# Queries and keys in five stages of seven block products for two groups, and a shorter rounding and closing step

## Chip, core and metric

The kernel runs on one core of one Trainium2 chip. The metric is device time in microseconds (us), as the median of several runs; lower is better. The core has five engines with a queue each: TensorE (PE) multiplies matrices into eight banks of PSUM, VectorE (DVE) and ScalarE (ACT) work element by element, GpSimd (POOL) does too but reaches no PSUM, and SyncE (SP) issues the transfers. An engine works through its queue in order; engines wait for each other on semaphores.

## What is computed

The input x has 32 batches of 32 rows with 512 columns. Each batch picks one of 16 conditions, whose 32x32 matrix mixes the batch's rows (h). On h runs causal attention with 32 query heads, 8 key and value heads and head size 128, with rotary positions. A second mixing and an fp8-rounded linear layer follow. Cut to what matters:

```python
h = einsum('bct,bcd->bdt', x, cond_weights[itok])
q, k, v = h @ wq, h @ wk, h @ wv                  # 32, 8 and 8 heads of 128
q = q*cos + rotate_half(q)*sin;  k likewise
att = softmax(mask(q @ k.T / sqrt(128)))          # four query heads share a key head
x = x + (att @ v) @ wo
y = einsum('bct,bcd->bdt', x, cond2_weights[itok])
s = amax(abs(y)) / 448;  a = fp8_round(y / s) * s # fp8 e4m3
f = a @ (fp8_round(qweight) * weight_scale).T + bias
so = amax(abs(f)) / 448
out = x + clip(f / so, -448, 448) * so
```

## The kernel before

**Layout.** The 1024 rows of x are 8 tiles of 128 rows, or two halves of 512 rows; `xacc` holds them to the end. The transposed h stands as `hT`. Every large product takes three passes of fp32r matmuls over a high and a low part of both operands (`_hi`, `_lo`: ACT rounds the high part, DVE or POOL subtracts it to get the low one); a pass over 128 contracted values and 512 columns is one matmul. All of them are issued at lines 733 to 735 (`three_pass`).

**Groups.** One key head with its four query heads is a group; there are eight. A group has two halves of program, `half(g, 0)` and `half(g, 1)`, written once for each engine. In a half PE makes the group's keys for 512 rows directly (`key`: 4 chunks x 3 passes = 12 matmuls), and two query heads for all 1024 rows as a 2x2 block product with seven block products in place of eight (`product` 0 to 6, 6 matmuls each; POOL sums the weight blocks in `sum_weights`; DVE joins the products in PSUM with seven `block_sum` steps). Each finished block of 128x512 (an item) is rotated: ACT swaps its halves (`swap`), DVE multiplies by cosine and sine (`rope`), POOL adds the two (`rope_add`). There are two `q_swap` buffers, so ACT's swap of item k+2 waits for POOL's addition of item k. Only one `wq_hi`/`wq_lo` set exists: while the products of a half run, ACT (`q_high`) and POOL (`q_low`) write the next half's seven parts over those already used.

**Attention.** `scores(g, r)` multiplies keys and queries of row half r once all items of the group have been added by POOL. DVE transposes them (`turn_scores`) and does the softmax in seven steps (`soft` 0 to 6, with ACT's `exponent` between 2 and 3); step 6 writes `p_tr`. `attend(g, r)` multiplies `p_tr` with the values, ACT and DVE split the outcome into `o_hi` and `o_lo` (`o_high`, `o_low`), and `project_out(g, r, j)` multiplies tile j of four with `wo` (12 matmuls), which DVE adds to `xacc` (`accumulate`). ACT and POOL split `wo` of a group (`wo_high`, `wo_low`, four heads) once the group before has been projected. One group and row half is a unit.

**Order.** The order in each queue is written out by hand, and the loop runs over groups 2 to 6. A half on PE is: key, attend of an older unit, seven products, three projected tiles of that unit, scores (second half of a group only), the fourth tile. While products of groups 0 and 1 run, the value product (`values`, 16 tiles) is still being finished and takes the place of projection. On DVE a half is: `soft` 0 to 2, the key's `rope`, four `o_low`, then block sums, `soft` 3 and 4, four ropes and the additions between each other, with `soft` 5 and 6 behind the last rope.

**The end.** After the last projection, `y_largest` finds the maximum of y, PE spreads it over partitions (`spread_max`), and for each of 8 tiles ACT scales y twice (`y_div`, `y_exp`), DVE turns `y_exp` into a power of two with bit operations (`magic`, line 1266), adds and subtracts it (lines 1286 and 1295, which rounds to fp8's steps), PE multiplies (`f_mm`) and DVE takes the maximum (`f_largest`). Then ACT divides each tile (line 652), DVE clips it (line 1319) and adds it back to `xacc` (line 1324), and SP stores it. `hold_clock` issues matmuls whose results nobody reads.

Of the kernel before, what the change touches and what calls it, by code (L numbers as in the profile page):

```python
# [7 lines left out]
F32 = mybir.dt.float32  # L8
# [19 lines left out]
ITEMS = 1 + REP  # L28
# [14 lines left out]
V_BEFORE = (9, 11, 15, 16)  # L43
# [35 lines left out]
def build(nc, x, itok, conds, wq, wk, wv, wo, qweight, w_scale, bias, consts, v_mem, out):  # L79
    with ExitStack() as ctx:  # L80
# [19 lines left out]
        with ExitStack() as products:  # L100
# [17 lines left out]
            with ExitStack() as steady:  # L118
                q_rot = sb("q_rot", [P, 2, REP, HALF], F32, steady)
                k_rot = sb("k_rot", [P, 2, HALF], F32, steady)  # L120
# [14 lines left out]
                wk_lo = sb("wk_lo", [P, KC, HD], F32R, steady)  # L135
# [3 lines left out]
                raw_q = sb("raw_q", [P, 2, KC, 2 * HD], F32, steady)  # L139
                raw_k = sb("raw_k", [P, KC, HD], F32, steady)  # L140
# [37 lines left out]
        dma_q = [sem(f"dma_q{i}") for i in range(2)]  # L178
        dma_k, dma_o, dma_out = sem("dma_k"), sem("dma_o"), sem("dma_out")
# [12 lines left out]
        w8_scaled, w8_step, wT_mm, wT_done = sem("w8_scaled"), sem("w8_step"), sem("wT_mm"), sem("wT_done")  # L192
        y_mm, y_copied, y_amax, tail_mm, tail_vec = (sem(n) for n in ("y_mm", "y_copied", "y_amax", "tail_mm", "tail_vec"))
        y_div_done, y_exp_done, y8_magic, y8_sum, y8_done = (
            sem(n) for n in ("y_div_done", "y_exp_done", "y8_magic", "y8_sum", "y8_done"))
# [26 lines left out]
        wv_raw = [raw_o[:], raw_q[:].rearrange("p s c n -> p (s c n)").rearrange("p (c n) -> p c n", n=HID)]  # L222
# [10 lines left out]
        bias_row = raw_k[0:BIAS_ROWS].rearrange("p c n -> p (c n)")  # L233
        bias_sc = k_rot[0:BIAS_ROWS, 0, :]
        bias_parts = wk_hi[0:BIAS_ROWS].rearrange("p c n -> p (c n)")
        y_div = lambda t: y_divs[:, t, :]
        y_exp = lambda t: wv_raw[1][:, t, :] if t < TPU else raw_o[:, t - TPU, :]
        f_div = y_exp
        f_keep = second_u[:]
        y_t = lambda t: y_kept[:, t, :] if t < TPU else y_ps[t][:]  # L240
        y_sum = [flat(p_tr), flat(s_nat[0])]
        tmp_scaled = [second_u[:], third_u[:]]
        tmp_sum = first_p[:]

        def left_part(h, i):

            a11, a12 = raw_q[:, h, 0:2, 0:HD], raw_q[:, h, 2:4, 0:HD]
            a22 = raw_q[:, h, 2:4, HD:2 * HD]
            return (a11, w_sum[:, 1], w_sum[:, 2], a12, w_sum[:, 0], a22, w_sum[:, 3])[i]

        def item_out(h, k):
            return k_rot[:, h, :] if k == 0 else q_rot[:, item_row[k - 1], 2 * h + item_head[k - 1], :]

        def unit_of(g, h):

            return (g - 2, 1) if h == 0 else (g - 1, 0)

        late = [range(V_BEFORE[n], V_BEFORE[n + 1]) for n in range(3)]

# [4 lines left out]
        def _(sp):  # L264

# [11 lines left out]
            sp.dma_start(raw_k[:], wk_v[:, :, 0:HD]).then_inc(dma_k, 16)  # L277
# [5 lines left out]

            def load_pair(g, h):
                sp.dma_start(raw_q[:, h], wq_v[:, :, bass.ds((2 * g + h) * 2 * HD, 2 * HD)]).then_inc(dma_q[h], 16)
# [7 lines left out]
            load_pair(0, 0)  # L293
            store_values(2)
            store_values(3)
            load_pair(0, 1)
# [6 lines left out]
            def half(g, h, last):  # L303

                n = 2 * g + h
                if not (isinstance(g, int) and g == KV - 1):
                    sp.wait_ge(wq_lo_done, PRODUCTS * (n + 1))
                    load_pair(g + 1, h)
                    if h == 0:
                        sp.wait_ge(wk_lo_done, g + 1)  # L310
                        sp.dma_start(raw_k[:], wk_v[:, :, bass.ds((g + 1) * HD, HD)]).then_inc(dma_k, 16)
                if h == 0 and not (isinstance(g, int) and g < 2):
                    sp.wait_ge(wo_lo_done, (g - 1) * REP)
                    sp.dma_start(raw_o[:], wo_v[:, bass.ds((g - 1) * REP, REP), :]).then_inc(dma_o, 16)
                if not (isinstance(g, int) and n < 2):
                    if not (isinstance(g, int) and n < 4):
                        sp.wait_ge(pv_mm, BPT * (n - 3))
                    load_values(g - 1, h)

            half(0, 0, None)  # L320
            for i in late[0]:
                store_values(i)
            half(0, 1, None)
            for i in late[1]:
                store_values(i)
            for i in range(V_SLOTS):
                sp.wait_ge(dma_v[i], 16 * len(range(i, V_BEFORE[2], V_SLOTS)))
            half(1, 0, None)
            for i in late[2]:
                store_values(i)  # L330
            for i in late[2]:
                sp.wait_ge(dma_v[i % V_SLOTS], 16 * (i // V_SLOTS + 1))
            half(1, 1, (0, 0))
            with sp.Fori(2, KV - 1) as g:
                half(g, 0, unit_of(g, 0))
                half(g, 1, unit_of(g, 1))
            half(KV - 1, 0, unit_of(KV - 1, 0))
            half(KV - 1, 1, unit_of(KV - 1, 1))

            sp.wait_ge(prod_mm, PRODUCTS * 2 * KV)  # L340
            sp.dma_start(raw_w8[:], qw_v).then_inc(dma_ffn, 16)
            sp.wait_ge(wk_lo_done, KV)
# [3 lines left out]
            for r in range(2):  # L346
                sp.wait_ge(pv_mm, BPT * (2 * (KV - 2) + r + 1))
                load_values(KV - 1, r)

            for t in range(TILES):  # L350
                sp.wait_ge(result, t + 1)
                sp.dma_start(out_rows[t], xacc[:, t, :]).then_inc(dma_out, 16)
# [4 lines left out]
        def _(pool):  # L357
            def sum_weights(g, h):

                n = 2 * g + h  # L360
                pool.wait_ge(dma_q[h], 16 * (g + 1))
                if isinstance(g, int) and n == 0:
# [3 lines left out]
                a11, a12 = raw_q[:, h, 0:2, 0:HD], raw_q[:, h, 2:4, 0:HD]  # L366
                a21, a22 = raw_q[:, h, 0:2, HD:2 * HD], raw_q[:, h, 2:4, HD:2 * HD]
# [7 lines left out]
            def q_low(g, h, i):  # L375
                n = PRODUCTS * (2 * g + h) + i
                pool.wait_ge(wq_hi_done, n + 1)
                pool.tensor_tensor(wq_lo[:, i], left_part(h, i), wq_hi[:, i].bitcast(F32), ALU.subtract).then_inc(wq_lo_done, 1)  # L378

# [21 lines left out]
            for i in range(PRODUCTS):  # L401
                q_low(0, 0, i)
# [957 lines left out]
```

## Time and profile before

| | |
|---|---|
| median of 3 runs | 521.12 us (521.07 to 521.58) |
| profiled execution, its own time | 521.22 us |
| its span, first to last instruction | 519.3 us |
| PE busy | 501.1 us (96%) |
| DVE busy | 418.6 us (81%) |
| POOL busy | 310.2 us (60%) |
| ACT busy | 248.2 us (48%) |
| TensorE clock granted, mean over the span | 0.991 |

The profiled execution took 0.10 us more than the median of the runs, and 1.92 us of its time lie outside the span. Busy counts time in which an instruction of the engine was under way; matmuls are pipelined, so the recorded length of one (about 390 ns) is longer than the distance between two.

### The profile page before, as it was taken

Reading aid. Unit: us, or ns where it says so; the run is one execution under the profiler, and the core shown is the slowest. Engines: PE = TensorE matmul, PEld = TensorE weight load, DVE = VectorE, ACT = ScalarE, POOL = GpSimd, SP = SyncE. Lnnn points to the kernel's source line nnn. Section 1 sums busy time; section 2 is a strip of 40 time slices with the busy share of each in tenths; the row PEclk is TensorE's granted clock in tenths of the full one; section 3 lists DMA queues with packets and bytes.
Section 4 is the critical chain, followed back from the end, with each engine's and each line's share of the span. In section 5 each row is a group of like instructions: output and inputs, shape, how many; then the busy total and the mean of one; then the engine's idle time right before and its main releaser. Section 6 shows DMA issues by size and latency. Waiting matters only on the chain.

```text
span 519.3 us, 9226 instructions
## 1 busy us (share of the span) xinstructions
PE 501.1 (96%) x3148; PEld 401.5 (77%) x3150; DVE 418.6 (81%) x662; ACT 248.2 (48%) x475; POOL 310.2 (60%) x308
## 2 busy tenths in 40 slices
PE   8999999999999999999999999999999999999990
PEld 6888888877888888888888888888888887788530
DVE  5468967899688877978797879787978798985896
ACT  2652644564446453735472637263726354232523
POOL 0668688888669746884788388838874754200000
PEclk9999999999999999999999999999999999999996
DMA  7346111320502050104010410131300014000004
GB/s 263 140 145 204 41 62 62 101 82 1 163 1 62 1 162 1 59 3 158 10 51 13 149 33 27 39 122 57 104 1 21 1 43 168 0 2 1 0 0 162
DMA packets 32644, 35.27 MB, mean 68 GB/s; under 512 B 2251, under 2 KB 22859, under 8 KB 32620
## 3 DMA queue, kind: packets, MB, share of 16 engines
q1 hardware_dynamic: 32620, 34.96, 21.1%
q8 instruction: 14, 0.23, 0.2%
q14 instruction: 10, 0.08, 0.0%
HBM read 28.66 MB, written 6.29 MB: 67 GB/s over the span
## 4 chain that ended last, share of the span: by engine, by line
PE 89%; DVE 4%; POOL 3%; issue 1%; DMA 1%; ACT 0%; DVEq 0%; ACTq 0%; SPq 0%; POOLq 0%
PE bank L733 23%; PE bank L734 22%; PE bank L735 22%; PE bank L803 3%; PE bank L792 3%; PE bank L705 3%; PE bank L706 3%; PE bank L707 3%; PE bank L676 1%; POOL q_rot L392 1%; PE bank L861 1%; PE bank L938 1%; POOL wq_lo L378 1%; PE bank L687 1%; DVE xacc L1324 1%
## 5 line engine op out<-in xcount | busy, mean ns | idle before, releaser
L392 POOL TENSOR_TENSOR q_rot<-q_rot,q_swap 128x512 f32<-128x512 f32 x64 | 88.2, 1377 | 60.9 <-DVE q_swap L1070 60.9
L521 ACT ACTIVATE q_swap<-bank 64x512 f32<-64x512 f32 x80 | 47.7, 596 | 124.3 <-PE bank L735 76.9
L733 PE MATMUL bank<-wo_hi,o_hi 128*128 128x512 f32 x256 | 101.4, 396 | 0.8 <-issue 0.6
L734 PE MATMUL bank<-wo_lo,o_hi 128*128 128x512 f32 x256 | 99.8, 390 | 0.0
L735 PE MATMUL bank<-wo_hi,o_lo 128*128 128x512 f32 x256 | 99.7, 390 | 0.0
L1118 DVE TENSOR_TENSOR xacc<-xacc,bank 128x512 f32<-128x512 f32 x64 | 43.7, 683 | 35.8 <-PE bank L735 35.7
L1070 DVE TENSOR_TENSOR q_swap<-q_swap,cst 128x512 f32<-128x512 f32 x80 | 60.2, 752 | 0.0
L733 PEld LDWEIGHTS bank<-wo_hi,o_hi 128*128 128x128 f32 x256 | 48.1, 188 | 13.1 <-issue 2.6
L735 PEld LDWEIGHTS bank<-wo_hi,o_lo 128*128 128x128 f32 x256 | 48.1, 188 | 10.2
L734 PEld LDWEIGHTS bank<-wo_lo,o_hi 128*128 128x128 f32 x256 | 48.1, 188 | 9.5
L387 POOL TENSOR_TENSOR wo_lo<-raw_o,wo_hi 128x512 fp32r<-128x512 f32 x32 | 45.5, 1444 | 9.5 <-ACT wo_hi L507 9.5
L733 PE MATMUL bank<-t_hi,wq_hi 128*128 128x512 f32 x128 | 49.9, 390 | 0.4 <-DVE o_lo L1111 0.4
L734 PE MATMUL bank<-t_lo,wq_hi 128*128 128x512 f32 x128 | 49.8, 389 | 0.0
L735 PE MATMUL bank<-t_hi,wq_lo 128*128 128x512 f32 x128 | 49.8, 389 | 0.0
L378 POOL TENSOR_TENSOR wq_lo<-w_sum,wq_hi 128x256 fp32r<-128x256 f32 x64 | 48.0, 761 | 1.6 <-ACT wq_hi L490 1.6
L522 ACT ACTIVATE q_swap<-bank 64x512 f32<-64x512 f32 x80 | 47.3, 591 | 0.9
L1069 DVE TENSOR_TENSOR q_rot<-bank,cst 128x512 f32<-128x512 f32 x64 | 43.9, 686 | 2.9 <-ACT q_swap L522 1.3
L378 POOL TENSOR_TENSOR wq_lo<-raw_q,wq_hi 128x256 fp32r<-128x256 f32 x48 | 38.4, 800 | 7.1 <-ACT wq_hi L490 7.1
L1111 DVE TENSOR_TENSOR o_lo<-bank,o_hi 128x512 fp32r<-128x512 f32 x64 | 39.6, 679 | 2.7 <-ACT o_hi L538 2.7
L392 POOL TENSOR_TENSOR k_rot<-k_rot,q_swap 128x512 f32<-128x512 f32 x16 | 20.8, 1298 | 34.1 <-DVE q_swap L1070 34.1
L538 ACT ACTIVATE o_hi<-bank 128x512 fp32r<-128x512 f32 x64 | 33.1, 604 | 16.4 <-PE bank L803 16.1
L733 PE MATMUL bank<-hT_hi,wq_hi 128*128 128x512 f32 x96 | 38.9, 405 | 0.0
(160 smaller groups left out, 1042.3 us busy)
## 6 DMA issues: line engine op xcount, KB each, us to landing
raw_q<-in_L_attn_wq SPq DMA_DIRECT2D x16, 512.0 KB, 4.0
raw_o<-in_L_attn_wo SPq DMA_DIRECT2D x8, 1024.0 KB, 7.0
v_st<-values SPq DMA_DIRECT2D x16, 256.0 KB, 4.4
xacc<-in_x SPq DMA_DIRECT2D x4, 512.0 KB, 7.5
raw_k<-in_L_attn_wk SPq DMA_DIRECT2D x8, 256.0 KB, 4.3
out<-xacc SPq DMA_DIRECT2D x8, 256.0 KB, 2.0
values<-v_more SPq DMA_DIRECT2D x6, 256.0 KB, 2.1
raw_o<-in_L_attn_wv SPq DMA_DIRECT2D x1, 1024.0 KB, 8.1
```

The costliest lines, as they stand in the source:

```text
L378: pool.tensor_tensor(wq_lo[:, i], left_part(h, i), wq_hi[:, i].bitcast(F32), ALU.subtract).then_inc(wq_lo_done, 1)
L387: pool.tensor_tensor(lo[:, h, :], raw_o[:, h, :], hi[:, h, :].bitcast(F32), ALU.subtract).then_inc(wo_lo_done, 1)
L392: pool.tensor_tensor(item_out(h, k), item_out(h, k), q_swap[(h + k) % 2][:], ALU.add).then_inc(rope_done, 1)
L521: act.activation(dst[0:P // 2, :], ps[P // 2:P, :], ACT.Copy)
L522: act.activation(dst[P // 2:P, :], ps[0:P // 2, :], ACT.Copy).then_inc(swap_done, 1)
L733: pe.matmul(dst, l_hi, r_hi, start=(i == 0), stop=False)
L734: pe.matmul(dst, l_hi, r_lo, start=False, stop=False)
L735: mm = pe.matmul(dst, l_lo, r_hi, start=False, stop=(i == n - 1))
L1069: dve.tensor_tensor(by_t(item_out(h, k)), by_t(item_ps[k][:]), cos_b, ALU.mult).then_inc(rope_cos, 1)
L1070: dve.tensor_tensor(by_t(q_swap[b][:]), by_t(q_swap[b][:]), sin_b, ALU.mult).then_inc(rope_mul, 1)
L1111: dve.tensor_tensor(by_batch(lo, b), by_tile(ps[b]), by_batch(hi, b).bitcast(F32), ALU.subtract).then_inc(o_lo_done, 1)
L1118: dve.tensor_tensor(xacc[:, tile, :], xacc[:, tile, :], w_ps[j % 2][:], ALU.add).then_inc(acc_done, 1)
```

## The change

Two groups now share five stages in place of four halves. A stage is one block product of seven with two heads' columns; the ten columns are eight query heads and the two keys, so `key`, `k_high` and `k_low` are gone. Stage 0 holds the even group's key (`k_first`) and its query head 0, stage 1 its heads 1 and 2, stage 2 its head 3 and the odd group's key (`k_second`), stages 3 and 4 the odd group's heads. `p` counts pairs of groups; the even group's scores follow in stage 2 (`side=0`), the odd group's in stage 4 (`side=1`). Attention and projection of older units are spread anew over the stages, stage 1 having no `attend`. `raw_q` has three slots, and stages 0 and 2 load their two columns with two transfers.

At the end ACT's absolute value, written as bfloat16, replaces the bit operations. Four f tiles are copied off PSUM early; PE adds `xacc` and the scaled result of tiles 2, 4 and 6 in PSUM with an identity matrix (`place_old`, `scaled_ident`) and ACT copies the sum to `xacc`; the clipping order and store order are written out anew. One `hold_clock` matmul stands where three stood.

```diff
-            for i in range(PRODUCTS):
-                q_low(0, 0, i)
-            k_low(0)
...
+            def stage(p, i, split_wo=None):
                 if more:
-                    sum_weights(*follow)
...
+                    sum_weights(*following(p, i))
+                if split_wo is not None:
                     for head in range(REP):
...
+                        wo_low(split_wo, head, wo_lo)
                 if more:
...
+                    for m in range(4):
+                        q_low(*following(p, i), m)
+                for k in range(ITEMS):
+                    rope_add(p, i, k)
                 if more:
...
+                    for m in range(4, PRODUCTS):
+                        q_low(*following(p, i), m)
+
+            def stages(p):
+                stage(p, 0)
+                stage(p, 1)
+                stage(p, 2, split_wo=None if isinstance(p, int) and p == 0 else 2 * p - 1)
+                stage(p, 3)
+                stage(p, 4, split_wo=2 * p)
...
+            def stage(p, i, last=None, fill=(), ahead=(), behind=(), end=(), side=None):
+                n = STAGES * p + i
+                for tile in ahead:
+                    project_out(*tile)
                 if last is not None:
-                    pe.wait_ge(rope_cos, 5 * n)
+                    pe.wait_ge(rope_cos, ITEMS * n)
+                    if i in (0, 3):
+                        pe.wait_ge(s_turned, 4 * p + (0 if i == 0 else 2) - 1)
                     attend(*last)
...
+                products_of(p, i, last)
+                for tile in fill:
+                    values(tile)
+                for tile in behind:
+                    project_out(*tile)
+                if side is not None:
+                    scores(p, side, 0)
+                    scores(p, side, 1)
+                for tile in end:
+                    project_out(*tile)
...
+                stage(p, 0, last=(2 * p - 2, 1), ahead=tiles(2 * p - 2, 0, 3), behind=tiles(2 * p - 2, 1, 0, 1))
+                stage(p, 1, behind=tiles(2 * p - 2, 1, 2, 3))
+                stage(p, 2, last=(2 * p - 1, 0), behind=tiles(2 * p - 1, 0, 0, 1, 2), side=0, end=tiles(2 * p - 1, 0, 3))
+                stage(p, 3, last=(2 * p - 1, 1), behind=tiles(2 * p - 1, 1, 0, 1, 2))
+                stage(p, 4, last=(2 * p, 0), ahead=tiles(2 * p - 1, 1, 3), behind=tiles(2 * p, 0, 0, 1, 2), side=1)
+
+            stage(0, 0, fill=late[0])
+            stage(0, 1, fill=late[1])
+            stage(0, 2, fill=late[2], side=0)
+            stage(0, 3, fill=late[3])
+            stage(0, 4, last=(0, 0), behind=tiles(0, 0, 0, 1, 2), side=1)
...
+                stage(p, 0, last=(2 * p - 2, 1), weights=(2 * p - 1, 0), steps=range(3), ahead=tiles(2 * p - 2, 0, 3),
+                      behind=tiles(2 * p - 2, 1, 0, 1))
+                stage(p, 1, weights=(2 * p - 1, 0), steps=range(3, SOFT_STEPS), behind=tiles(2 * p - 2, 1, 2, 3))
...
+            stage(0, 3, weights=(0, 0), fill=late[3])
...
-            def magic(t):
...
-                dve.tensor_scalar(y_exp(t).bitcast(I32), y_exp(t).bitcast(I32), EXP_BITS, HALF_BIT,
-                                  ALU.bitwise_and, ALU.bitwise_or).then_inc(y8_magic, 1)
...
+                    pe.matmul(f_ps[n + 1][:, part], ident, xacc[:, BY_PE[n], part], start=(c == 0), stop=False)
...
+                    mm = pe.matmul(f_ps[n + 1][:, part], scaled_ident, f_div(t)[:, part], start=False, stop=(c == KC - 1))
```

The first `stage` is POOL's, the second (from `last=None, fill=()` on) PE's, the calls with `weights` DVE's. `late` holds value tiles 9 and 10, 11 and 12, 13 and 14, 15 for the stages (0, 0) to (0, 3). The softmax of unit (2p-1, 0) is split: `soft` 0 to 2 in stage 0 and 3 to 6 in stage 1. That of unit (0, 0), which stood whole at the end of `half(0, 1)`, is spread over stage (0, 3).

The first place is DVE's queue where a part of the program ends with a softmax (`xacc` rows are `accumulate`, `p_tr` is `soft` 6, `s_nat1` rows the next unit's `soft` 0 to 2, bank6 and bank7 the two banks of projection). Before, from the last rope of `half(7, 0)` to the start of the next half:

```order
L1069 TENSOR_TENSOR q_rot<-bank4,cst 128x512
L1070 TENSOR_TENSOR q_swap0<-q_swap0,cst 128x512
L1098 TENSOR_TENSOR s_nat0<-s_exp,s_rec 128x512
L1118 TENSOR_TENSOR xacc<-xacc,bank7 128x512
L1105 STREAM_TRANSPOSE p_tr<-s_nat0 128x512
L1118 TENSOR_TENSOR xacc<-xacc,bank6 128x512
...
L1086 TENSOR_TENSOR s_nat1<-s_nat1,cst 128x512
```

Of the change, from the last rope of stage 1 of the last pair to the start of stage 2:

```order
L1098 TENSOR_TENSOR q_rot<-bank4,cst 128x512
L1099 TENSOR_TENSOR q_swap1<-q_swap1,cst 128x512
L1127 TENSOR_TENSOR s_nat0<-s_exp,s_rec 128x512
L1147 TENSOR_TENSOR xacc<-xacc,bank7 128x512
L1134 STREAM_TRANSPOSE p_tr<-s_nat0 128x512
L1115 TENSOR_TENSOR s_nat1<-s_nat1,cst 128x512
```

The rows up to `p_tr` are alike, but the bank7 row now takes in the last projected tile of its unit, and PE's next work is the `attend` that reads `p_tr`; before, two more tiles (the bank6 row and another) and a key stood between on PE.

The second place is POOL's queue ahead of the rope additions (rows that write `q_rot`, `k_rot` or `k_second`). Before, in `half(g, 1)` of the loop:

```order
L373 TENSOR_TENSOR w_sum<-raw_q,w_sum 128x256
...
L387 TENSOR_TENSOR wo_lo<-raw_o,wo_hi 128x512
...
L392 TENSOR_TENSOR k_rot<-k_rot,q_swap1 128x512
...
L378 TENSOR_TENSOR wq_lo<-raw_q,wq_hi 128x256
...
L392 TENSOR_TENSOR q_rot<-q_rot,q_swap0 128x512
```

Of the change, in stage 2 of the last pair:

```order
L415 TENSOR_TENSOR w_sum<-raw_q,w_sum 128x256
L424 TENSOR_TENSOR wo_lo<-raw_o,wo_hi 128x512 x4
L419 TENSOR_TENSOR wq_lo<-raw_q,wq_hi 128x256
L419 TENSOR_TENSOR wq_lo<-w_sum,wq_hi 128x256 x2
L419 TENSOR_TENSOR wq_lo<-raw_q,wq_hi 128x256
L428 TENSOR_TENSOR q_rot<-q_rot,q_swap0 128x512
L428 TENSOR_TENSOR k_second<-k_second,q_swap1 128x512
```

Before, two `wo_lo` stood on either side of the key's addition, and three additions in a row came behind the first of a query head. Now all four `wo_lo` and four `wq_lo` stand ahead of the first of four additions.

## Rows read from the trace of the kernel before

**Rows 1.** The page: span, then busy time of each engine.

```profile
span 519.3 us, 9226 instructions
PE 501.1 (96%) x3148; PEld 401.5 (77%) x3150; DVE 418.6 (81%) x662; ACT 248.2 (48%) x475; POOL 310.2 (60%) x308
```

**Rows 2.** Windows: stretch, length, busy PE, PEld, DVE, ACT, POOL; clock, DMA, GB/s.

```profile
46.24:129.12 82.88, 82.25 (x497) 66.92 (x495) 70.22 (x103) 43.31 (x84) 67.55 (x67) 1.00 0.22 68
...
231.19:282.19 51.00, 51.00 (x334) 41.72 (x333) 42.50 (x67) 26.01 (x51) 36.35 (x38) 1.00 0.18 57
```

**Rows 3.** Timeline of PE, `half(g, 1)` in the loop: start, length, instruction.

```profile
261.23 1.17 PE L803 MATMUL bank<-p_tr,v_st 32*128 32x128 f32 x32
262.33 0.50 PE L733 MATMUL bank<-hT_hi,wq_hi 128*128 128x512 f32 x1
...
271.99 0.39 PE L733 MATMUL bank<-wo_hi,o_hi 128*128 128x512 f32 x1
...
280.24 1.96 PE L792 MATMUL bank<-q_rot,k_rot 128*32 128x128 f32 x64
```

**Rows 4.** Timeline of DVE in that half (in brackets idle time and releaser).

```profile
268.11 0.70 DVE L1050 TENSOR_TENSOR bank<-bank,first_p 128x512 f32<-128x512 f32 x1 [0.19 <-PE bank L735]
...
277.25 0.69 DVE L1070 TENSOR_TENSOR q_swap<-q_swap,cst 128x512 f32<-128x512 f32 x1
...
279.07 0.70 DVE L1105 STREAM_TRANSPOSE p_tr<-s_nat 128x512 f32<-128x512 f32 x1
```

**Rows 5.** Timeline of POOL in that half.

```profile
260.66 2.99 POOL L387 TENSOR_TENSOR wo_lo<-raw_o,wo_hi 128x512 fp32r<-128x512 f32 x2
...
265.79 2.56 POOL L387 TENSOR_TENSOR wo_lo<-raw_o,wo_hi 128x512 fp32r<-128x512 f32 x2 [0.23 <-ACT wo_hi L507]
268.31 0.74 POOL L378 TENSOR_TENSOR wq_lo<-raw_q,wq_hi 128x256 fp32r<-128x256 f32 x1
269.01 1.43 POOL L378 TENSOR_TENSOR wq_lo<-w_sum,wq_hi 128x256 fp32r<-128x256 f32 x2
...
272.17 1.29 POOL L392 TENSOR_TENSOR q_rot<-q_rot,q_swap 128x512 f32<-128x512 f32 x1 [1.03 <-DVE q_swap L1070]
...
278.02 1.68 POOL L392 TENSOR_TENSOR q_rot<-q_rot,q_swap 128x512 f32<-128x512 f32 x1 [0.63 <-DVE q_swap L1070]
```

**Rows 6.** Timeline of DVE ahead of the first key.

```profile
47.86 2.89 DVE L1001 TENSOR_TENSOR t_lo<-t_full,t_hi 128x1024 fp32r<-128x1024 f32 x2
```

**Rows 7.** Timeline of DVE in the rounding of y and the closing step.

```profile
498.17 0.68 DVE L1286 SCALAR_TENSOR_TENSOR s_nat<-raw_o,y_divs 128x512 f32<-128x512 f32 x1
498.77 0.42 DVE L1266 TENSOR_SCALAR raw_o<-raw_o 128x512 int32<-128x512 int32 x1
499.10 0.69 DVE L1295 SCALAR_TENSOR_TENSOR y<-raw_o,s_nat 128x512 bf16<-128x512 f32 x1
...
500.31 0.68 DVE L1286 SCALAR_TENSOR_TENSOR p_tr<-raw_o,y_divs 128x512 f32<-128x512 f32 x1
...
508.49 1.00 DVE L1319 TENSOR_SCALAR raw_q<-raw_q 128x512 f32<-128x512 f32 x2 [0.79 <-ACT raw_q L652]
...
515.40 1.41 DVE L1324 SCALAR_TENSOR_TENSOR xacc<-raw_o,col,xacc 128x512 f32<-128x512 f32 x2
```

**Rows 8.** DMA issues: size, us to landing.

```profile
raw_q<-in_L_attn_wq SPq DMA_DIRECT2D x16, 512.0 KB, 4.0
...
out<-xacc SPq DMA_DIRECT2D x8, 256.0 KB, 2.0
```

**Rows 9.** Windows in the closing step, columns as in rows 2.

```profile
517.00:518.00 1.00, 0.00 (x0) 0.00 (x0) 0.00 (x0) 0.00 (x0) 0.00 (x0) 0.50 1.00 373
```

**Rows 10.** Windows around PE's last matmul.

```profile
506.70:510.20 3.50, 0.00 (x0) 0.00 (x0) 2.44 (x8) 2.46 (x5) 0.00 (x0) 1.00 0.00 0
510.20:519.30 9.10, 0.00 (x0) 0.00 (x0) 6.60 (x13) 2.31 (x4) 0.00 (x0) 0.50 0.61 231
```

**Rows 11.** Timeline of PE at the start of the program.

```profile
1.46 4.28 PE L664 MATMUL bank<-warm 128*128 128x512 bf16 x11 [1.46 <-DVE warm L946]
```

More of the change, by code:

```diff
@@ L243, in build @@
         tmp_sum = first_p[:]
[L245 to L258, printed above, removed]
+        SLOT = (0, 1, 0, 1, 2)
@@ L334, in _ @@
[L334 to L340, printed above, removed]
+            stage(0, 4)
+            with sp.Fori(1, PAIRS - 1) as p:
+                for i in range(STAGES):
+                    stage(p, i)
+            for i in range(STAGES):
+                stage(PAIRS - 1, i)
+            sp.wait_ge(prod_mm, PRODUCTS * STAGES * PAIRS)
@@ L597, in _ @@
+            stage(0, 0)
+            stage(0, 1)
+            stage(0, 2)
+            stage(0, 3, soft=(0, 0))
+            stage(0, 4, last=(0, 0), soft=(0, 1), split_wo=0)
+            with act.Fori(1, PAIRS - 1) as p:
+                stages(p)
+            stages(PAIRS - 1)
             for b in range(BPT):
@@ L1118, in accumulate, with stage, soft_part @@
                 dve.tensor_tensor(xacc[:, tile, :], xacc[:, tile, :], w_ps[j % 2][:], ALU.add).then_inc(acc_done, 1)
-            def half(g, h, last=None, weights=None, fill=(), fill_last=(), soft_first=None):
-                def soft_part(*steps):
-                    if weights is not None:
-                        for step in steps:
+            def stage(p, i, last=None, weights=None, steps=range(SOFT_STEPS), fill=(), ahead=(), behind=(), end=(), side=None):
+                def soft_part(*some):
+                    for step in some:
+                        if weights is not None and step in steps:
                             soft(*weights, step)
-                def add_out(j):
-                    if last is not None:
-                        accumulate(*last, j)
                 soft_part(0, 1, 2)
-                rope(g, h, 0)
+                for tile in ahead:
+                    accumulate(*tile)
                 if last is not None:
@@ L1183, in round_w8 @@
+            dve.wait_ge(dma_const, 32)
+            stage(0, 0, fill=late[0])
+            stage(0, 1, fill=late[1])
+            stage(0, 2, fill=late[2], side=0)
+            stage(0, 3, weights=(0, 0), fill=late[3])
+            stage(0, 4, last=(0, 0), weights=(0, 1), behind=tiles(0, 0, 0, 1, 2), side=1)
+            with dve.Fori(1, PAIRS - 1) as p:
+                stages(p)
+            stages(PAIRS - 1)
             def round_w8(c):
```

618 lines of the change are left out of this document (301 added, 317 removed).

## The prediction

> **What bounds the kernel now.** The page first: PE is busy for 501.1 of 519.3 us and DVE for 418.6 [rows 1], so PE is full and DVE is next. Then the windows: a group of the loop takes 51.00 us and PE is busy for all of them; in the opening, from the first key to the tile behind group 1's scores, PE idles for 0.63 of 82.88 us [rows 2]. So a matmul less is time less, unless PE then waits. Third the timelines of one half of the loop, from which I take the durations and, more important, how far the other engines trail PE. I call P the start of a stage's first product, 262.33 in that half.
>
> PE [rows 3]: an `attend` of 32 small matmuls holds it for 1.1 us (261.23 to 262.33). The seven products, 42 matmuls, take 9.66 (262.33 to 271.99), 0.23 each. Three projected tiles take 8.25 (271.99 to 280.24), 2.75 each. So scores start at P+17.91.
>
> DVE [rows 4]: its third block sum still waits for PE at 268.11, P+5.78. From there 19 more instructions stand with hardly a gap between them, at about 0.60 from start to start, up to `soft` 6, which begins at 279.07 and lasts 0.70: `p_tr` is ready at P+17.44. The sine of the last rope stands at 277.25, P+14.92.
>
> POOL [rows 5]: the four query additions run from 272.17 (P+9.84) to 279.70 (P+17.37), 7.53 us, since each pair of `q_swap` buffers goes round through POOL, ACT and DVE. A first addition that is late therefore makes the last one late by as much. The last one ends 0.54 us ahead of the scores.
>
> Today both are covered: behind `p_tr` PE has two tiles and a key (in the first half of a group), or scores, a tile and the next key. The question is what covers them in the new order.
>
> **Removed.** 16 halves of 54 matmuls become 20 stages of 42: 864 less 840, 24 matmuls, at 0.23 that is 5.5 us, or 1.38 for each of the four pairs of groups.
>
> **Added and hidden.** 28 block sums at 0.60 are 17 us more of DVE, some 4.2 in a pair of groups; POOL gets 28 `wq_lo` and 16 weight sums at 0.70 (from 268.31 to 269.01 [rows 5]), less 8 `wk_lo`. In the loop DVE is busy for 42.5 of 51.0 and POOL for 36.4 [rows 2], so neither becomes full, and this costs nothing as busy time; it matters where it stands in a queue, below. Two 256 KB loads replace one of 512 KB that lands in 4.0 us [rows 8]; they are issued a stage (over 15 us) ahead and stay hidden even at twice that.
>
> **Waits in a steady pair (p = 1 to 3).** Stage 1 has no `attend` and only two tiles: PE has 9.66 + 5.50 = 15.16 us of work, then comes the `attend` that reads the `p_tr` of this same stage. DVE's rows up to `soft` 6 are the same as before, so it ends at P+17.44 at the earliest: PE waits 2.3, with the signal 2.4. Lower bound 1.7, if one 0.60 step less is in the way; upper bound 3.5, if POOL's additions are late here too. Behind this `attend` everything of PE is queued.
>
> Stage 2: POOL comes from the last addition of stage 1 (P+17.37 there), about as `attend` starts, and has three `wq_lo` (2.1), four weight sums (2.8 at the same 0.70), four `wo_low` at 1.28 (5.1, half of 265.79's 2.56) and four `wq_lo` (2.8) ahead of the first addition: 12.8, so to P+11.6 of stage 2 after 1.1 of `attend`. The natural time is P+9.84. The last addition ends at 11.6 + 7.53 = P+19.1, and PE is at the scores at P+17.9: 1.2. Bounds 0 (if the loop's slack of 1.76 took it up) and 2.4 (contended, rival C).
>
> Stage 4: the same POOL work, with a tile of 2.75 ahead of `attend`, but the splitting of `wo` may only start behind that tile. Between 0 and 1.2; I take 0.9, since the start of the splitting moves back as well. In the last pair no next weights stand ahead, so there it is 0. Stages 0 and 3 use a `p_tr` from a stage earlier: no wait.
>
> So 2.4 + 1.2 + 0.9 - 1.38 = +3.1 for a pair, three pairs less the last 0.9: **+8.4**.
>
> **Waits in the opening (pair 0).**
> - Product 1 of stage (0, 0) reads the third part of `t_lo`. Two parts take 47.86 to 50.75 [rows 6], so the third ends at about 49.3. Before, PE began at 46.24 [rows 2] with a key (12 x 0.23 = 2.8) and product 0 (1.4), so product 1 came at 50.4. Now product 1 comes at 47.6: 1.7.
> - Stage (0, 2): products and two value tiles take 15.16, then scores want POOL's last addition of this stage, P+17.37: 2.2.
> - The first product of stage (0, 3) uses the bank of the second scores and waits for DVE's transpose of it (0.70 and a signal): 0.9, where a projected tile lies between otherwise.
> - Stage (0, 3): products and one value tile, 12.41. Then `attend(0, 0)` wants `soft` 6 of this stage. One DVE step fewer than in the row's half stands ahead of it, so P+16.8: **4.4**, the largest single wait.
> - Stage (0, 4): POOL is 0.5 later against `attend` than in stage 2, so 1.8 at the scores by the same sum.
>
> Together 11.0, less 1.38 and the 0.6 that PE idles there today: **+9.0** (bounds +5 and +11, with 0 and 2.4 for the POOL waits and 2.5 to 5 for the 4.4).
>
> **The end.** DVE makes a y tile in 2.14 (498.17 to 500.31), of which the bit operation is 0.33 (498.77 to 499.10) [rows 7]. Without it over six tiles on the path: -2.0. ACT's absolute value takes the place of a pass that it made already, and the bfloat16 input has no row; I take DVE's 0.60 for it as for fp32 (half of it would give 4 us more over the end). In the closing step DVE now has seven or eight clips and five additions in place of eight and eight, 0.33 and 0.67 (1.00 a tile from 508.49 to 515.40), so its last result is some 4.5 earlier in all. But the stores: 256 KB at 373 GB/s [rows 9] is 0.70, six of eight are then queued behind each other, and each lands in 2.0 [rows 8]. The end moves from 519.3 to about 516.3: **-3.0**, with bounds of -1.5 and -5.
>
> **Sum.** 519.3 + 9.0 + 8.4 - 3.0 = 533.7 span, + 1.92 outside = 535.6 us for the profiled execution; the median of runs lay 0.10 below it, so 535.5.
>
> **Rivals.** *A*, the sum above.
>
> *B, the clock.* PE's last matmul ends at 506.7, the granted clock stays at 1.00 (2.4 GHz) to 510.2 and is then 0.50 (1.2 GHz) [rows 10]. The wait of 4.4 in stage (0, 3) is longer than these 3.5 us. The 11 first matmuls of the program took 4.28 us [rows 11] where 11 at 0.23 are 2.5: a fall costs about 1.8. Then 537.3. The Trainium skill ("TensorE: Matmul & The Clock Gate", Part 1) calls the throttled clock the default that activity releases; rows 10 agree. Against B: at the end nothing follows at all, while here PE stands between dense stages.
>
> *C, POOL slower.* At 260.66 two `wo_lo` took 2.99 in place of 2.56, and the addition at 278.02 took 1.68 in place of 1.29, while DVE worked on two SBUF operands [rows 5]. If all POOL work of stages 2, 4 and (0, 4) is 1.17 times as long, 12.8 becomes 15.0: +2.2 at three stages 2, two stages 4 and (0, 4), less what the bounds above leave free, some 1.2 each: +7, 542.5. The Trainium skill ("GPSIMD Engine Reference", section 1) says that POOL's SBUF interfaces are shared with VectorE and that instructions with two SBUF inputs contend; the 1.68 beside 1.29 agrees.
>
> *D, faster: DVE does not trail.* The chain of 20 DVE instructions starts at P+5.8 behind the third block sum and would be short enough: without `soft` 0 to 2 and `o_low` ahead of it in stages 1 and (0, 3), and with POOL's additions in step, each wait falls below what PE's work covers. Then only -5.5, the t_lo wait and the end count: 521.1 - 5.5 + 1.7 - 3.0 = 514.3. It decides if the waits, 24 in my sum (11.0 + 3 x 4.5 - 0.9), come to less than 8.5. Against it: 19 of 20 steps stand gapless at 0.60 in rows 4 although PE's sums were ready; that is what P+17.4 is made of.
>
> *E, no change:* waits of just 8.5; nothing speaks for that in particular.
>
> **Chances.** A 0.63 (530 to 540 for itself), B 0.14, C 0.08, D 0.11, E 0.04. The range 526 to 541 takes in A's bounds (opening +5, pairs with only the 2.4 left, end -5: about 524; upper bounds about 541) and B, and leaves out D and most of C. 0.2%, 1 us, is about what a measurement of this kernel can tell from no change: faster 0.11, same 0.04, slower 0.85.
>
> **What would show it.** Right: PE busy falls by some 5 us while the span grows; waits of PE's first `attend` matmuls for DVE's `p_tr`, 4.4 once at stage (0, 3) to (0, 4) and 2.4 in each later pair; waits of the scores for POOL's `q_rot`, `k_second`; a pair of groups taking about 105 in place of 102.0. Wrong: `soft` 6 of stage 1 ending before P+15.2, POOL's first addition of stage 2 at P+10, a granted clock under 1.00 before the end, or stores of the end that leave DMA idle between them.

## The result and the profile after

| | before | changed |
|---|---|---|
| median | 521.35 us (521.07 to 521.74, 4 runs) | 550.51 us (547.80 to 550.80, 4 runs) |
| profiled execution | 521.22 us, span 519.3 | 547.80 us, span 546.0 |

The changed kernel takes 1.0549 times as long (95% interval 1.052 to 1.0578). Slower was forecast, but by half of that: 535.5 us, with 541 as the upper bound. The profiled execution is the fastest of the changed kernel; the others had a mean granted clock of 0.969 to 0.974 where this one has 0.979, so the rows below show rather too little of the loss. All sums here are made against the profiled execution.

From the page of the changed kernel (as [rows 1], with the granted clock in 40 slices):

```profile
span 546.0 us, 9233 instructions
PE 509.6 (93%) x3160; PEld 408.1 (75%) x3160; DVE 429.6 (79%) x676; ACT 259.2 (47%) x505; POOL 334.1 (61%) x344
PEclk9999999889999799999998999999989999999999
```

PE has 24 matmuls of the products fewer (in the closing step the trace has 48 small ones more and 12 of `hold_clock` fewer) and is yet busy for 8.5 us longer: the slices of 8 and 7 in the clock's line hold the stretches in which it ran at half speed. Where the time went is read off the start of the odd groups' scores. In the timeline of PE before, group 1's and group 7's:

```profile
127.24 1.96 PE L792 MATMUL bank<-q_rot,k_rot 128*32 128x128 f32 x64
...
433.24 1.95 PE L792 MATMUL bank<-q_rot,k_rot 128*32 128x128 f32 x64
```

and of the changed kernel, of groups 1, 3, 5 and 7:

```profile
139.74 1.95 PE L800 MATMUL bank<-q_rot,k_second 128*32 128x128 f32 x64
...
248.10 1.95 PE L800 MATMUL bank<-q_rot,k_second 128*32 128x128 f32 x64
...
356.34 1.96 PE L800 MATMUL bank<-q_rot,k_second 128*32 128x128 f32 x64
...
463.08 1.95 PE L800 MATMUL bank<-q_rot,k_second 128*32 128x128 f32 x64
```

PE's first matmul for keys and queries starts at 46.24 in the profiled executions of both. So the opening is 12.5 us longer (forecast 9.0). The pairs of groups take 108.4, 108.2 and 106.7 in place of 102.0: +6.4, +6.2 and +4.7 (forecast 3.1, 3.1 and 2.2). From the last scores to the end there are 82.9 in place of 86.1 us: -3.1 (forecast -3.0). Together 26.7, which is the difference of the spans.

The waits of PE in the changed kernel (line and tile that waited, who released it: us in all, times, longest):

```profile
PE bank L811 <- DVE p_tr L1134: 13.5, 4, 4.6
PE bank L748 <- DVE xacc L1147: 6.1, 5, 1.7
PE bank L800 <- POOL q_rot L428: 3.4, 1, 3.4
```

The first row is the `attend` behind stage 1 of each later pair and that behind stage (0, 3). The second is not in the forecast: a projected tile that waits until DVE has taken the tile before last out of its bank. The third is group 0's scores. On PE they look like this (timeline; in brackets the idle time and its releaser):

```profile
95.97 3.19 PE L800 MATMUL bank<-q_rot,k_first 128*32 128x128 f32 x64 [3.37 <-POOL q_rot L428]
...
117.14 2.09 PE L811 MATMUL bank<-p_tr,v_st 32*128 32x128 f32 x32 [4.61 <-DVE p_tr L1134]
...
178.75 2.09 PE L811 MATMUL bank<-p_tr,v_st 32*128 32x128 f32 x32 [2.87 <-DVE p_tr L1134]
...
245.03 0.50 PE L748 MATMUL bank<-wo_hi,o_hi 128*128 128x512 f32 x1 [1.25 <-DVE xacc L1147]
```

These two `attend` take 2.09 us; in [rows 3] it took 1.17. The windows around those places (columns as in [rows 2], the granted clock third from the end) show why:

```profile
96.00:100.00 4.00, 3.17 (x64) 2.70 (x64) 1.50 (x3) 0.00 (x0) 3.86 (x6) 0.57 0.36 99
117.00:121.00 4.00, 3.86 (x38) 3.36 (x39) 3.83 (x5) 1.78 (x4) 3.86 (x5) 0.57 0.02 4
178.00:184.00 6.00, 5.25 (x40) 4.34 (x41) 5.93 (x9) 2.33 (x5) 5.84 (x8) 0.54 0.26 79
184.00:186.00 2.00, 2.00 (x8) 1.57 (x7) 0.07 (x2) 2.00 (x5) 1.51 (x2) 0.69 0.62 170
186.00:192.00 6.00, 6.00 (x28) 4.96 (x27) 4.64 (x9) 3.98 (x9) 6.00 (x7) 1.00 0.01 3
```

The clock goes to its lower level, 1.2 GHz, behind each of the waits for `p_tr` and behind that of group 0's scores, and comes back some 3 to 7 us later. That happens five times ahead of the end, once in each pair and twice in the opening, not at most once as in the forecast.

POOL from stage 1 to stage 2 of pair 1 (timeline, as [rows 5]):

```profile
176.96 1.65 POOL L428 TENSOR_TENSOR q_rot<-q_rot,q_swap 128x512 f32<-128x512 f32 x1 [0.63 <-DVE q_swap L1099]
...
184.93 5.06 POOL L424 TENSOR_TENSOR wo_lo<-raw_o,wo_hi 128x512 fp32r<-128x512 f32 x4 [0.49 <-ACT wo_hi L528]
189.93 0.76 POOL L419 TENSOR_TENSOR wq_lo<-raw_q,wq_hi 128x256 fp32r<-128x256 f32 x1
190.63 1.46 POOL L419 TENSOR_TENSOR wq_lo<-w_sum,wq_hi 128x256 fp32r<-128x256 f32 x2
192.04 1.21 POOL L419 TENSOR_TENSOR wq_lo<-raw_q,wq_hi 128x256 fp32r<-128x256 f32 x1
193.20 1.30 POOL L428 TENSOR_TENSOR q_rot<-q_rot,q_swap 128x512 f32<-128x512 f32 x1
```

From the end of stage 1's last addition (178.6) to stage 2's first (193.2) POOL works for 14.6 us with hardly a gap, where the forecast put 12.8.

### The profile page after: what moved, and what is told of

It reads as the page before. It is cut to its first block, busy times and chain, and to the rows that moved or that the text cites. A ratio compares the mean times of both kernels' runs of the same rounds, so it can differ in the third digit from the quotient of the medians.

```text
span 546.0 us, 9233 instructions
## 1 busy us (share of the span) xinstructions
PE 509.6 (93%) x3160; PEld 408.1 (75%) x3160; DVE 429.6 (79%) x676; ACT 259.2 (47%) x505; POOL 334.1 (61%) x344
## 4 chain that ended last, share of the span: by engine, by line
PE 50%; POOL 21%; DVE 13%; issue 11%; ACT 2%; DMA 1%; POOLq 0%; DVEq 0%; ACTq 0%; SPq 0%
PE bank L748 13%; PE bank L750 12%; PE bank L749 12%; POOL q_rot L428 8%; POOL wq_lo L419 6%; DVE q_swap L1099 4%; PE bank L800 3%; POOL wo_lo L424 3%; PE bank L811 2%; PE bank L720 2%; PE bank L722 2%; PE bank L721 1%; ACT q_swap L538 1%; PE bank L691 1%; DVE q_rot L1098 1%
## 5 line engine op out<-in xcount | busy, mean ns | idle before, releaser
L419 POOL TENSOR_TENSOR wq_lo<-raw_q,wq_hi 128x256 fp32r<-128x256 f32 x60 | 48.5, 809 | 34.1 <-ACT wq_hi L517 34.1
L419 POOL TENSOR_TENSOR wq_lo<-w_sum,wq_hi 128x256 fp32r<-128x256 f32 x80 | 63.7, 806 | 2.2 <-ACT wq_hi L517 2.1
L748 PE MATMUL bank<-t_hi,wq_hi 128*128 128x512 f32 x160 | 63.1, 394 | 1.0 <-DVE t_lo L1031 1.0
L749 PE MATMUL bank<-t_lo,wq_hi 128*128 128x512 f32 x160 | 62.8, 392 | 0.0
L750 PE MATMUL bank<-t_hi,wq_lo 128*128 128x512 f32 x160 | 62.6, 391 | 0.0
L1099 DVE TENSOR_TENSOR q_swap<-q_swap,cst 128x512 f32<-128x512 f32 x80 | 61.8, 772 | 0.0
L748 PE MATMUL bank<-hT_hi,wq_hi 128*128 128x512 f32 x120 | 50.0, 417 | 0.9 <-issue 0.9
L424 POOL TENSOR_TENSOR wo_lo<-raw_o,wo_hi 128x512 fp32r<-128x512 f32 x32 | 41.4, 1328 | 14.8 <-ACT wo_hi L528 14.8
L749 PE MATMUL bank<-hT_lo,wq_hi 128*128 128x512 f32 x120 | 48.5, 404 | 0.0
L750 PE MATMUL bank<-hT_hi,wq_lo 128*128 128x512 f32 x120 | 48.0, 400 | 0.0
```

What stands on the lines that cost most here:

```text
L419: pool.tensor_tensor(wq_lo[:, m], left_part(i, m), wq_hi[:, m].bitcast(F32), ALU.subtract).then_inc(wq_lo_done, 1)
L424: pool.tensor_tensor(lo[:, h, :], raw_o[:, h, :], hi[:, h, :].bitcast(F32), ALU.subtract).then_inc(wo_lo_done, 1)
L748: pe.matmul(dst, l_hi, r_hi, start=(i == 0), stop=False)
L749: pe.matmul(dst, l_hi, r_lo, start=False, stop=False)
L750: mm = pe.matmul(dst, l_lo, r_hi, start=False, stop=(i == n - 1))
L1099: dve.tensor_tensor(by_t(q_swap[b][:]), by_t(q_swap[b][:]), sin_b, ALU.mult).then_inc(rope_mul, 1)
```

## The experiments

Two theories stood at the start. The first is the forecast's: the late `p_tr` costs its wait, and as the clock now shows, a fall of the clock besides; take it away and both come back. The second: another queue, POOL's or DVE's, sets the length of a pair, and a wait that is removed comes back elsewhere. Unless it is said otherwise, a kernel below computes all that the changed kernel does and differs by the lines shown. The comparisons are with the kernel before, run on the same chip.

**e1: the softmax early**

```diff
+                if i == 1:
+                    for step in early:
+                        soft(*weights, step)
                 soft_part(0, 1, 2)
...
                 block_sum(p, i, 0)
+                if i == 3:
+                    for step in early:
+                        soft(*weights, step)
                 block_sum(p, i, 1)
...
-                stage(p, 1, weights=(2 * p - 1, 0), steps=range(3, SOFT_STEPS), behind=tiles(2 * p - 2, 1, 2, 3))
+                stage(p, 1, weights=(2 * p - 1, 0), steps=range(3, SOFT_STEPS), early=range(3, SOFT_STEPS), behind=tiles(2 * p - 2, 1, 2, 3))
```

> DVE does soft 3 to 6 of unit (2p-1, 0) as the first thing in stage 1, where it idles for 2.0 us at present, and those of unit (0, 0) behind the first block sum of stage (0, 3); nothing else changes. If p_tr at the end of DVE's queue is what PE waits for, and the clock's falls come from that wait, then the waits of 3.0, 3.0 and 3.3 us in the loop shrink to the 0.7 us by which the last rope's cosine trails PE's tiles, the one of 4.8 us to about 2.7, and the slow attend and products behind them (1.6 to 3.0 us each) go: 550.5 becomes about 535 us. If DVE or POOL are simply too busy (the rival), the wait comes back at the accumulation or at the scores, and the time stays over 546.

Measured: 550.92 us, 1.0555 times before (1.0538 to 1.0573): nothing gained. Yet the wait for `p_tr` is gone, as the timeline of PE in pair 1 shows, from the end of stage 1 on (the last row is in stage 4):

```profile
180.53 1.17 PE L811 MATMUL bank<-p_tr,v_st 32*128 32x128 f32 x32 [1.10 <-DVE q_rot L1098]
...
185.37 0.49 PE L748 MATMUL bank<-t_hi,wq_hi 128*128 128x512 f32 x1 [0.72 <-DVE o_lo L1140]
...
193.93 0.49 PE L748 MATMUL bank<-wo_hi,o_hi 128*128 128x512 f32 x1 [1.47 <-POOL wo_lo L424]
...
201.45 0.50 PE L748 MATMUL bank<-wo_hi,o_hi 128*128 128x512 f32 x1 [1.79 <-DVE xacc L1147]
...
248.71 0.50 PE L748 MATMUL bank<-wo_hi,o_hi 128*128 128x512 f32 x1 [1.26 <-DVE xacc L1147]
```

and so is the fall of the clock, in the window of the same kernel:

```profile
178.00:184.00 6.00, 4.90 (x49) 3.82 (x48) 5.90 (x9) 3.97 (x9) 4.58 (x5) 1.00 0.00 0
```

PE arrives in stage 2 earlier and waits there three times, 4.0 us together, for `o_low`, `wo_low` and the accumulation. A pair still takes 108.5 us (scores at 143.27 and 251.78). The first theory falls: the wait and the fall were real, but something behind them was as late. POOL, in the same kernel:

```profile
180.96 1.28 POOL L428 TENSOR_TENSOR q_rot<-q_rot,q_swap 128x512 f32<-128x512 f32 x1 [0.65 <-DVE q_swap L1099]
...
196.90 1.28 POOL L428 TENSOR_TENSOR q_rot<-q_rot,q_swap 128x512 f32<-128x512 f32 x1
```

From 182.2 to 196.9 it is 14.7 us again. POOL's way from stage 1 to stage 2 is as long as before, though `p_tr` is early.

**e2: filler in the waits**

```diff
+            def hold(p, i):
+                first = isinstance(p, int) and p == 0
+                count = {2: 14, 3: 20}.get(i, 0) if first else {1: 13}.get(i, 0)
+                if count:
+                    pe.wait_ge(first_kept, STAGES * p + i + 1)
+                for _ in range(count):
+                    pe.matmul(a_ps[:], hT_hi[:, 0, 0:P], hT_hi[:, 0, 0:HALF], start=True, stop=True)
...
                 for tile in behind:
                     project_out(*tile)
+                hold(p, i)
                 if side is not None:
```

> PE gets matmuls whose results nobody reads where it waits: 13 at the end of each later stage 1, 14 ahead of group 0's scores and 20 at the end of stage (0, 3), about as long as each wait. No order changes. If the clock falls because PE idles there, the granted clock stays at 1.00 up to the end and attend and products behind the waits take 1.1 and 9.65 us again: 7 to 9 us less, 542 to 543, with all waits on DVE still there in the form of filler. If the falls have another cause, the time stays at 550, or grows where the filler is longer than the wait.

Measured: 550.63 us, 1.0543 times before (1.051 to 1.0576). The windows of the first two pairs, with a clock of 0.97 and 0.98 in the changed kernel, now have:

```profile
145.00:250.00 105.00, 101.12 (x643) 81.88 (x647) 85.66 (x135) 53.73 (x108) 76.39 (x79) 1.00 0.17 50
250.00:360.00 110.00, 106.14 (x699) 85.53 (x692) 90.50 (x141) 53.74 (x108) 81.96 (x86) 1.00 0.17 53
```

So the falls do come from PE's idleness (the Trainium skill, "TensorE: Matmul & The Clock Gate", Part 1, says that activity releases the throttle; the trace agrees). Where a wait has no filler the clock still falls, so in stage 2 of the last pair behind 2.4 us for the accumulation:

```profile
414.00:418.00 4.00, 2.26 (x5) 1.82 (x6) 4.00 (x7) 1.81 (x4) 2.20 (x2) 0.67 0.01 2
```

But the 7 to 9 us didn't come, and a pair takes 108.3 to 108.6 us: without the fall PE is at stage 2's accumulation sooner and waits there for 2.3 to 2.4 us in place of none to 1.0. The same lesson from the other side.

**e3: the additions first**

```diff
-                if more:
+                if more and i not in (2, 4):
                     for m in range(4):
                         q_low(*following(p, i), m)
                 for k in range(ITEMS):
                     rope_add(p, i, k)
                 if more:
-                    for m in range(4, PRODUCTS):
+                    for m in range(0 if i in (2, 4) else 4, PRODUCTS):
                         q_low(*following(p, i), m)
```

> In stages 2 and 4 POOL does all seven wq_lo behind the four rope additions in place of four ahead of them. If late additions hold up the accumulation behind the third rope, and that holds PE's third projected tile, then these waits (1.8, 1.4, 1.2, 1.4 and 1.1 us, together 6.9) go: about 544. If the splitting of wo alone makes the additions late, less than 2 us changes; if the weight parts are then late for the next stage, products wait and the time grows.

Measured: 542.70 us, 1.0406 times before (1.0389 to 1.0423): 8 us less than the changed kernel, as the second theory has it. The row of waits for `xacc` is gone; that for `p_tr` stands at 13.5 us as before. The scores of groups 1, 3, 5 and 7 in its timeline:

```profile
137.08 1.96 PE L800 MATMUL bank<-q_rot,k_second 128*32 128x128 f32 x64
...
244.17 1.95 PE L800 MATMUL bank<-q_rot,k_second 128*32 128x128 f32 x64
...
348.67 1.96 PE L800 MATMUL bank<-q_rot,k_second 128*32 128x128 f32 x64
...
455.93 1.96 PE L800 MATMUL bank<-q_rot,k_second 128*32 128x128 f32 x64
```

107.1, 104.5 and 107.3 us. Pairs 1 and 2 run the same lines of the loop, so they differ by chance, and their windows say in what. Behind the wait of pair 1, and behind that of pair 2:

```profile
176.00:182.00 6.00, 5.91 (x41) 4.91 (x42) 5.32 (x8) 2.98 (x6) 5.63 (x7) 0.50 0.33 97
...
283.00:287.00 4.00, 3.81 (x44) 3.21 (x45) 3.93 (x6) 2.62 (x6) 3.92 (x6) 1.00 0.01 4
```

Both waits are 2.9 us long. Behind one of them the clock fell, and that pair is 2.6 us longer. I take this as the price of a fall where POOL doesn't cover it.

**e4: the old stages with the new end**

To the kernel before come all lines of the change for the end, and none for the stages. Of the edit, whose core stands in the diff ahead of the prediction:

```diff
-                    hold_clock(f_ps[t][:], 3)
+                    pe.wait_ge(y_exp_done, t + 1)
+                    hold_clock(f_ps[t][:], 1)
...
-            for t in range(TILES):
-                sp.wait_ge(result, t + 1)
+            for t in STORE_ORDER:
+                if t in BY_PE:
```

> The groups of the kernel before with the end of the change. From the last scores to the last instruction the change took 81.0 us where the kernel before took 84.2. If that part stands by itself, 521.3 becomes 518.2 and it is the only part of the change that gains; if it owed something to the stages ahead of it, less.

Measured: 518.39 us, 0.9934 times before (0.9918 to 0.9951). Its last scores start at 433.89 and its span is 516.8: 82.9 us, as in the changed kernel. The end is worth 3.1 us of its own, and this is the fastest of all kernels here.

**e5: both orders, and e6: the additions first, with filler**

e5 has the lines of e1 and e3, e6 those of e2 and e3.

> The softmax steps early (as in e1) and the additions first (as in e3) in one kernel. e1 showed no gain, since POOL's work between the last addition of stage 1 and the first of stage 2, 14.7 us, stayed what it was and held the accumulation in stage 2; e3 took that work out of the way but kept the late p_tr. If the two stand one behind the other, each hiding the other, both together give more than e1 and e3 add up to (0 and 8): the clock stays at 1.00 in the loop, the wait at the end of stage 1 is 1.1 us, those at the accumulations are gone, a pair takes about 102 us in place of 108.3, and the time is about 530. If e1's steps cost DVE as much as they save, it stays at e3's 542.7.

> The additions first (as in e3) and filler matmuls in the waits (as in e2), so that the late p_tr stays and only the clock's falls go. e2 gave nothing, though the clock was at 1.00 in the loop, because POOL set the pace of stage 2. If the falls cost time where POOL does not, this takes 1.5 to 3 us less than e3 for each fall, some 6 together: about 537. If they cost nothing of their own, it stays at 542.7.

Measured: e5 536.53 us (1.0298, interval 1.0278 to 1.0318), e6 535.44 us (1.0272, 1.0252 to 1.0292). Together the two orders gain 14 us where alone they gained 0 and 8, so each did hide the other. Filler gains 7.3 us from e3 to e6 where it gained nothing in e2: with POOL's `wq_lo` out of the way the falls do cost time, as e6 expected. But the expected 102 us for a pair didn't come. In e5 and in e6 the scores of groups 1 and 3:

```profile
137.74 1.95 PE L800 MATMUL bank<-q_rot,k_second 128*32 128x128 f32 x64
...
242.42 1.96 PE L800 MATMUL bank<-q_rot,k_second 128*32 128x128 f32 x64
```

```profile
136.46 1.95 PE L800 MATMUL bank<-q_rot,k_second 128*32 128x128 f32 x64
...
241.20 1.95 PE L800 MATMUL bank<-q_rot,k_second 128*32 128x128 f32 x64
```

104.7 in both, although one waits 1.1 us for a rope's cosine at the end of stage 1 and the other stands there for 3.1 us under filler. It is also the 104.5 of e3's pair without a fall. So a wait of 3 us for `p_tr` costs nothing here as long as the clock stays up, and a third thing sets the pair. In e5 PE's first projected tile of stage 2 names it:

```profile
188.41 0.49 PE L748 MATMUL bank<-wo_hi,o_hi 128*128 128x512 f32 x1 [1.49 <-POOL wo_lo L424]
```

and POOL in e5 ends the four `wo_low` just then:

```profile
175.42 1.28 POOL L428 TENSOR_TENSOR q_rot<-q_rot,q_swap 128x512 f32<-128x512 f32 x1 [0.65 <-DVE q_swap L1099]
...
182.70 5.49 POOL L424 TENSOR_TENSOR wo_lo<-raw_o,wo_hi 128x512 fp32r<-128x512 f32 x4
```

**e7: the sums behind the additions too, and e8: filler in the opening**

e7 is e5 with this on POOL, and with ACT's `q_high` 0 to 6 behind its four swaps in stages 2 and 4; e8 adds e2's `hold` to it, with the second count line.

```diff
-                if more:
+                if more and i not in (2, 4):
                     sum_weights(*following(p, i))
...
                 if more:
+                    if i in (2, 4):
+                        sum_weights(*following(p, i))
                     for m in range(0 if i in (2, 4) else 4, PRODUCTS):
                         q_low(*following(p, i), m)
...
-                count = {2: 14, 3: 20}.get(i, 0) if first else {1: 13}.get(i, 0)
+                count = {2: 13, 3: 12}.get(i, 0) if first else 0
```

> As e5, and in stages 2 and 4 POOL also does the four weight sums behind the additions, and ACT the high parts of the next weights behind its swaps. e5 and e6 both end at 104.7 us for a pair, one with and one without the wait for p_tr, so something else sets it: by the theory POOL's way from the last addition of stage 1 over three wq_lo (2.9), four sums (2.9) and four wo_low (5.5) to the first projected tile of stage 2, for which PE waits 1.5 in e5. Without the sums that tile has its wo_low some 2.9 us earlier: no wait for wo_low, a pair takes 103.0 to 103.5, the time 531 to 533. If DVE's o_low and ropes set the pair, it stays at 104.7 and 536.5; if the weights are late for stages 3 and 0, it grows.

> e7 and filler in the two longest waits of the opening alone: 13 matmuls ahead of group 0's scores, 12 ahead of the attend at the start of stage (0, 4). In e5 the granted clock is below 1.00 only there and at the end. If each fall costs what slow matmuls behind it take longer (0.9 + 1.3 us at stage (0, 4), about 1 at the scores), this takes 2 to 3 us less than e7; if POOL covers it here too, the same.

Measured: e7 531.04 us (1.0175, 1.0158 to 1.0192). Its scores of groups 1 and 3, and the window from one to the other:

```profile
136.88 1.96 PE L804 MATMUL bank<-q_rot,k_second 128*32 128x128 f32 x64
...
240.06 1.96 PE L804 MATMUL bank<-q_rot,k_second 128*32 128x128 f32 x64
```

```profile
136.88:240.06 103.18, 101.31 (x660) 82.14 (x659) 89.97 (x139) 53.51 (x108) 79.15 (x84) 1.00 0.19 57
```

A pair takes 103.2 us, as the theory said, and the wait for `wo_low` is gone. e8 takes 529.42 us (1.0152, 1.0135 to 1.0169). Its profiled execution began its first product 6 us later than that of e7, so I take its opening from there: 88.0 us from the first product to group 1's scores, in e7 90.6. That is 2.6 less, the upper half of what was expected; of the medians it is 1.6, less than expected. It is the price of one fall and not of two: in e7 group 0's scores wait only 1.7 us and run at full speed, and just `attend(0, 0)` is slow, as its timeline shows.

```profile
94.27 1.96 PE L804 MATMUL bank<-q_rot,k_first 128*32 128x128 f32 x64 [1.67 <-POOL q_rot L428]
...
115.16 2.09 PE L815 MATMUL bank<-p_tr,v_st 32*128 32x128 f32 x32 [4.25 <-DVE q_rot L1102]
```

## Why the prediction was wrong

**Removed, added and hidden; the end.** The count of matmuls and the end were right: -3.1 for the end against -3.0, and e4 shows it alone. Its terms fit too: from the first multiplication of a y tile to that of the last it is 2.1 us less (forecast 2.0), and DVE's last result comes 4.3 us earlier after the last scores (4.5). With all that the orders of e7 take away, a pair has 103.2 us, 1.2 more than before. PE is busy for 101.3 of them, where it was for all of the 102.0: that is 0.7 less and not 1.38, for a reason that no run here shows. The idle 1.9 are e7's waits between stages 1 and 2, 1.1 for the last rope's cosine and 0.7 for `o_low`.

**Stage 1's wait** was right as a wait: 2.9 to 3.1 us measured for 2.4. The step that failed is what was made of it, "So 2.4 + 1.2 + 0.9 - 1.38 = +3.1 for a pair". This adds the wait for `p_tr` and that for POOL, as if one stood behind the other on PE alone. Between stages 1 and 2 of the changed kernel POOL hardly waits, 0.5 us for ACT's `wo_high`, so the two run side by side, and the later one decides. e1 takes the wait for `p_tr` away and e2 the falls behind it, and both gain nothing. By itself, adding would have made the forecast too high. What made it too low are POOL's terms, 1.2 and 0.9: with `p_tr` early, in e1, POOL's lateness still holds PE for 4.5 us in pair 1, 1.47 for `wo_low`, which the sum didn't have, and 1.79 and 1.26 for the accumulations. e3 shows that the accumulations wait because of POOL's `wq_lo`, and e7 that `wo_low` is late because of its sums.

**Stage 2 and stage 4.** The mechanism was right, POOL's work ahead of the first addition, and e3 shows it. The size was off, "12.8, so to P+11.6": it is 14.6, since two of the `wq_lo` and a sum took 1.1 to 1.2 in place of 0.74, `wo_high` held it for 0.5, and the sums have small gaps that the sum of 0.70 each left out. That is rival C's 15.0, to which I gave 0.08. The place was off too. The scores don't wait: the late addition holds ACT's swap, the swap the rope, and behind the third rope DVE's queue has the accumulation that frees a bank. So the wait stands one tile ahead of the scores. In the last pair it came in stage 2, as in the forecast, and not in stage 4.

**The clock.** The sum took A, without one, and B had one, for 1.8 us. There were five ahead of the end. The price of 1.8 for one was too low beside the 2.6 that e3 shows. The window of pair 1 of the changed kernel, from scores to scores, shows what the sum put at nothing:

```profile
139.74:248.10 108.36, 104.18 (x659) 84.54 (x659) 89.83 (x141) 53.97 (x108) 80.00 (x84) 0.97 0.18 55
```

PE idles there for 4.2 us, near the 4.5 of the sum's waits, but is busy for 104.2 and not for 102.0 less 1.38. Yet in the changed kernel itself the pairs' falls mostly lie beside POOL's lateness, which e2 shows by getting nothing for removing them: PE then idles for POOL instead. They become dear once POOL is out of the way.

**Faster, if DVE doesn't trail** (rival D): it does. `soft` 6 of stage 1 ran from 178.0 to 178.7 where PE had its tiles done at 175.9, even with DVE idle for 2 us at the head of the stage; and where e1 makes `p_tr` early, the last rope still comes 1.1 us late.

**The opening** was 12.5 for 9.0. `attend(0, 0)` waited 4.6 (forecast 4.4) and group 0's scores 3.4 (2.2). Product 1 waited 1.0 for `t_lo` (1.7). In all, the waits there come to 11.6 (11.0). The rest of the excess is the two falls, in the scores of group 0, which take 3.19 in place of 1.96, and in `attend(0, 0)` with the matmuls behind it; e8 puts the second at 1.6 to 2.6.

**What a pair of the change is made of**, by the kernels in turn: 108.3 in the changed kernel; 104.7 with the additions first and the clock up (e5, e6); 103.2 with the sums moved and the softmax early (e7); 102.0 before. So of the 6.3 us that a pair lost, 3.6 are POOL's `wq_lo` ahead of the additions and the falls, and 1.5 its sums (with ACT's `q_high`, which e7 moves too; no run parts the two). The 1.2 that stay no run here removed, nor 7.0 of the opening, which takes 88.0 us in e8 and took 81.0 before. For the opening the cause is not settled: e7 waits there 1.0 for `t_lo`, 1.7 for POOL's last addition, 2.1 for `wq_lo` at the head of stage (0, 3) and 4.3 for the last rope ahead of `attend(0, 0)`, and I tried no other order of the value tiles.

## What to carry to other kernels

When work is packed so that PE needs less time, write down for each other queue how long it takes from the last hand-over of one stage to the first of the next; the longest of these sets the stage, and waits on PE that lie beside the same stretch of that queue are not added but the largest is taken. Test a suspected wait by removing it and looking where PE waits next: here a removed wait of 3 us came back whole, in the next stage. Put what the next consumer needs ahead of what only the next stage needs, in each queue.

## What the runs showed of the hardware

The granted clock fell to its lower level behind waits of PE of 2.4 to 4.6 us in the middle of dense work, though at the end of the kernel before it stayed at 1.00 for 3.5 us without a matmul [rows 10], and behind two waits in e3, 2.8 ahead of group 0's scores and 2.9 in pair 2, it didn't fall at all. POOL and DVE slow each other down both ways: in stage 2 of the changed kernel a `wq_lo` that starts at 192.04 takes 1.21 in place of 0.74, beside DVE's multiplication by the sine at 191.96, which takes its usual time; the next such multiplication takes 1.28 in place of the 0.69 of [rows 4], beside POOL's addition at 193.20, which takes its usual 1.30. Both times the one that began later is the longer one, as these rows of DVE's timeline and POOL's further up show. The Trainium skill ("GPSIMD Engine Reference", section 1) has the two share their SBUF interfaces, and all four are instructions with two SBUF inputs; the rows agree.

```profile
191.96 0.68 DVE L1099 TENSOR_TENSOR q_swap<-q_swap,cst 128x512 f32<-128x512 f32 x1
...
193.76 1.28 DVE L1099 TENSOR_TENSOR q_swap<-q_swap,cst 128x512 f32<-128x512 f32 x1
```
